# Attention on one core: VectorE's copy of the transposed x before another small block, two sets of small steps on later tiles

## What is computed

```python
q, k, v = x @ Wq, x @ Wk, x @ Wv                      # x: 16 sequences of 512 rows, 128 wide
latent_kv = (k + v) @ W_down_kv
k_rec, v_rec = latent_kv @ W_up_k, latent_kv @ W_up_v
scores = (q_heads @ k_heads.T) * scale                # 512 x 512 for each of 16 heads
scores = scores * exp(-1e-4 * |i - j|)
out = softmax(scores) @ v_heads
return concat_heads(out) @ Wo
```

## Time and profile before

| what | us |
|---|---|
| median of 3 runs | 1317.2 |
| lowest and highest | 1317.09, 1326.12 |
| the profiled execution, its own time | 1316.34 |
| its span, first to last instruction | 1314.3 |
| mean granted TensorE clock | 0.968 of full speed |

### The profile page before, as it was taken

One profiled execution on the slowest core, in us unless ns is written; L12 is line 12 of the kernel. 1 busy time (PEld: TensorE's weight loads), 2 busy tenths in 40 slices (PEclk: granted clock), 3 DMA queues, 4 the chain that ended last, 5 costly groups with the idle time before them and its releaser, 6 DMA issues. The chain is left out here.

```text
span 1314.3 us, 27474 instructions
## 1 busy us (share of the span) xinstructions
PE 1172.5 (89%) x7406; PEld 524.3 (40%) x7406; DVE 940.5 (72%) x2964; ACT 928.4 (71%) x1411; POOL 653.5 (50%) x1101
## 2 busy tenths in 40 slices
PE   4979999999999999996899749899969999999995
PEld 1222222222222222222566549577733443434442
DVE  5676777777777776776688766566466888888764
ACT  3878999999999999996665671445535666666554
POOL 5435555555555666423555540234233566666534
PEclk7999999999999999998999969899989999999998
DMA  5664565555566554511960003000000000000001
GB/s 155 138 122 88 90 115 108 105 103 105 104 116 114 110 105 96 103 34 59 236 193 11 1 5 125 1 1 0 0 0 1 9 9 16 16 8 17 9 17 33
DMA packets 71699, 87.96 MB, mean 67 GB/s; under 512 B 10368, under 2 KB 65190, under 8 KB 66022
## 3 DMA queue, kind: packets, MB, share of 16 engines
q1 hardware_dynamic: 69326, 85.81, 30.9%
q10 hardware_dynamic: 2296, 1.25, 0.4%
HBM read 63.84 MB, written 31.59 MB: 73 GB/s over the span
## 5 line engine op out<-in xcount | busy, mean ns | idle before, releaser
L562 ACT ACTIVATE a_probs<-a_S 128x1024 f32<-128x1024 f32 x512 | 496.8, 1037 | 53.7 <-DVE a_S L708 46.2
L708 DVE TENSOR_TENSOR a_S<-a_S,a_tables 128x256 f32<-128x256 f32 (+1 forms) x512 | 281.3, 561 | 149.1 <-PE a_S L578 146.1
L585 PE MATMUL a_O<-a_probs,a_V 128*32 128x512 f32 x2048 | 275.9, 611 | 2.4 <-ACT a_probs L562 0.6
L578 PE MATMUL a_S<-a_Qs,a_Ks 48*128 48x512 bf16 x1024 | 180.8, 390 | 15.8 <-ACT a_probs L562 10.5
L578 PEld LDWEIGHTS a_S<-a_Qs,a_Ks 48*128 48x128 bf16 x1024 | 42.7, 93 | 231.5 <-ACT a_probs L562 195.0
L2276 ACT ACTIVATE e_hid<-e_H 128x512 f32<-128x512 f32 x128 | 69.5, 595 | 57.6 <-PE e_H L2391 57.6
L455 POOL CAST a_parts<-a_whole 128x512 bf16<-128x512 f32 x45 | 27.5, 612 | 151.7 <-DVE a_whole L718 151.7
L1962 ACT ACTIVATE g_hid<-g_H,w_b 128x512 f32<-128x512 f32 x64 | 44.0, 687 | 57.9 <-PE g_H L1996 57.9
L2389 PE MATMUL e_H<-e_gated,w_We 64*128 64x512 f32 x256 | 73.2, 648 | 1.3 <-ACT e_hid L2276 1.2
L585 PEld LDWEIGHTS a_O<-a_probs,a_V 128*32 128x32 f32 x2048 | 40.5, 108 | 82.9 <-issue 67.8
L2400 PE MATMUL e_O<-e_hid,w_We 128*64 128x512 f32 x256 | 68.7, 609 | 0.4 <-ACT e_hid L2276 0.4
(11 more groups left out here) (405 smaller groups left out, 2382.1 us busy)
## 6 DMA issues: line engine op xcount, KB each, us to landing
a_parts_dram<-a_parts SPq DMA_DIRECT2D x94, 192.0 KB, 5.5
a_Qs<-a_parts_dram SPq DMA_DIRECT2D x60, 192.0 KB
m_taps_by_step<-h_taps SPq DMA_DIRECT2D x8, 1024.0 KB, 13.6
m_taps<-m_taps_by_step SPq DMA_DIRECT2D x8, 1024.0 KB, 5.1
a_Qs<-a_parts_dram SPq DMA_DIRECT2D x60, 128.0 KB
a_Ks<-a_parts_dram SPq DMA_DIRECT2D x30, 192.0 KB
a_Qs<-a_parts_dram SPq DMA_DIRECT2D x68, 64.0 KB
XY<-L_attn_x SPq DMA_DIRECT2D x16, 256.0 KB, 7.2
```

Source lines behind the costliest of these rows:

```text
L562: act.activation(probs[n % KEPT][:], S[n % RING][:], ACT.Exp).then_inc(exped, 1)
L578: mm = pe.matmul(S[n % RING][:, par, :], Ks[p][rows, pr, kb * P:(kb + 1) * P], Qs[p][Q_OF(kb)][rows, pr, :], start=True, stop=True)
L585: mm = pe.matmul(O[VC * j:VC * (j + 1), :], V[q][:, kb, HG * g + j, :], probs[(2 * m + j // 2) % KEPT][:, j % 2, :], start=(kb == 0), stop ...
L708: v.tensor_tensor(s[:, :, where], s[:, :, where], wide, ALU.mult).then_inc(corrected, 1)
```

## The change

On VectorE, within a batch: the copy of xT is done after the correction of tile 19 in place of tile 20; the small steps of `joined` move from tile 19 to tile 28; the four `bn_stats` of `next_norm`, with the wait ahead of them, move from tile 21 to tile 24, where its small steps follow them at once. No instruction is added or removed, and no other engine's order is touched.

```diff
@@ -873,11 +873,9 @@
                         out_norm.moments_of(v, t - 1, None, p=1 - p)
                     if n == 11 and (not isinstance(t, int) or t >= 2):
                         out_norm.moments_of(v, t - 2, None, p=p)
-                    if n == 21 and (not isinstance(t, int) or t >= 2):
+                    if n == 24 and (not isinstance(t, int) or t >= 2):
                         out_norm.wait_added(v, t - 2)
-                        next_norm.moments_of(v, t - 2, X[:, t - 2], only_stats=True, p=p)
-                    if n == 24 and (not isinstance(t, int) or t >= 2):
-                        next_norm.moments_of(v, t - 2, None, core.xmean, p=p)
+                        next_norm.moments_of(v, t - 2, X[:, t - 2], core.xmean, p=p)
                     if n in (16, 22, 31):
                         g = (n - 16) // 6
                         invert(at(f"OT{g}"), g, t * 2 + 1 if g == 0 else None)
@@ -887,10 +885,10 @@
                     if n == 18 and ahead and (not isinstance(t, int) or t < B - 3):
                         v.wait_ge(later[1 - p], (t - p) * 8 + 32)
                         joined.moments_of(v, t + 3, X[:, t + 3], only_stats=True, p=1 - p)
-                    if n == 19 and ahead and (not isinstance(t, int) or t < B - 3):
+                    if n == 19 and ahead:
+                        take(at("xT"), xnT[:])
+                    if n == 28 and ahead and (not isinstance(t, int) or t < B - 3):
                         joined.moments_of(v, t + 3, None, core.in_mean, p=1 - p)
-                    if n == 20 and ahead:
-                        take(at("xT"), xnT[:])
                     if n == 25 and ahead:
                         scale_queries(at("q"), t + 2)
                     if n == 29 and ahead:
```

## The result

The changed kernel took 1311.18 us (median of 8 runs, 1309.06 to 1313.5). The kernel before, run beside it, took 1323.17 us (median of 8, 1317.09 to 1326.21). The ratio is 0.9925, with a 95% interval from 0.9905 to 0.9945. The change makes the kernel faster, by 10 to 12 us (the ratio says 9.9, the two medians are 12.0 apart) and less than 1%. Two later comparisons of the same pair gave 0.991 (0.9882 to 0.9939) and 0.9921 (0.9891 to 0.995). The forecast was 11.9 us, 0.9%, and 1305.3 us. That time is 5.9 us too low: it rested on a median of three runs of the kernel before, 1317.2, and the median of eight was 6.0 us higher.

The account below looks back on a forecast made before the run. Prediction: no engine fills a batch; engines waiting for each other in a ring lose some 2.6 us of it. 2.6 + 9.9 + 0.2 - 0.8 = 11.9 us gave 1305.3 us for the median; range 1301.5 to 1311.5.

Parts of the forecast that it names:

- Batches 2 to 12: Copy one tile ahead and small steps away from tile 19: 0.90 us a batch, 9.9 us in eleven batches.
- The stall: TensorE's 1.20 us wait before OT1 (L601) in batch 7 for the copy of xT, claimed to go whole.
- the ring: Score, correction, exponential, and three tiles on the next score: claimed to limit score 24's gain to 0.82 to 0.90 us.
- The statistics at tile 24: Block of 1.54 to 1.7 us ahead of correction 25, claimed covered by the q projection with 0.3 to 0.5 us spare.
- Batches 14 and 15: No q projection, so no cover for the statistics block: 0.4 us lost in each, 0.8 in all.
- Batches 13, 0 and 1: Batch 13 gains 0.2 us; batch 0's gain is lost to batch 1's key wait; batch 1 gains 2.6 us.
- Its low clock: Batch 1's 3.41 us at clock 0.50 behind its 2.31 us stall, claimed to go, worth 1.7 us.
- rival 1: Start of batch 2: second low stretch, 111.65 to 115.06, goes too, about 1.4 us more, 1303.9 us; chance 0.20.
- All behind the attention is unchanged and starts sooner by the same amount: Layers after the attention: claimed to pass the 11.9 us gain on unchanged.
- The absolute time: Whole kernel: profiled execution 1304.4 us, plus 0.9 for the median of the runs, 1305.3 us.
- rival 3: Ring bound elsewhere, only small steps leaving tile 19 count: eleven times 0.6 less 0.8, 5.8 us, 1311.4; chance 0.12.
- rival 4: Statistics block ahead of correction 25 becomes the bound: 14 times 0.4, 5.6 us lost, 1322.8 us; chance 0.05.

Follow-up runs that it names:

- swap: Against the kernel before: copy of xT to tile 19 and small steps of `joined` to tile 20, statistics as before; 1315.61 us, ratio 0.9941.
- small_only: Against the kernel before: only the small steps of `joined` moved to tile 28, copy at tile 20, statistics at tile 21; 1309.9 us, ratio 0.9932.
- stats_only: Against the kernel before: only the statistics of `next_norm` moved from tile 21 to tile 24; 1323.17 us, ratio 1.003.
- before_b: The kernel before run again, nothing changed; profiled execution 1319.76 us, ratio to the kernel before 0.9996.
- before_c: The kernel before run a third time, nothing changed; profiled execution 1317.43 us, ratio to the kernel before 1.0.
- stats_kept: Against the changed kernel: statistics of `next_norm` left at tile 21, their small steps at tile 24; 1309.51 us, ratio 0.9907.
- stats_twice: Against the changed kernel: four more bn_stats that nothing reads, ahead of the statistics at tile 24; 1321.46 us, ratio 1.0002.
- q_later: Against stats_kept: q projection behind score 25 instead of 24, scaling of the queries split over tiles 26 and 27; 1316.52 us, ratio 0.9958.

## Why the prediction was right or wrong

**Batches 2 to 12: right.** Eleven times 0.90 was forecast, 9.9 us. Batches 3 to 11 are shorter by 0.88 to 0.91, batch 12 by 0.76, batch 2 by 0.88 against the profiles that have no low stretch in it: 9.7 us. The stall goes whole, score 24 is then late by ScalarE, and score 25 follows after TensorE's own work, as walked; swap (stall gone, half the gain) and small_only (stall shortened, most of the gain) tell the ring from the stall.

**The statistics at tile 24: covered, but the term was mis-sized.** "Ends at 318.14 to 318.30 ... with 0.3 to 0.5 us to spare" was wrong: the block measured 1.94 us to the end of its last step in the changed kernel (308.85 to 310.79), and the same in stats_only, where correction 25 starts 1.88 us after it begins; VectorE was idle 0.09 us before correction 25 of the changed kernel. It cost nothing in the changed kernel, 0.15 us a batch in stats_only. The fault was to take the length from a row outside the loop, where the block is 0.34 us shorter.

**Batches 14 and 15: direction right, size too large.** 0.4 us each was forecast, 0.25 and 0.23 measured. Exponential 25 did come 0.41 us later (a step of 1.31 in place of 0.90 us), but 0.18 of it came back before exponential 31 (a step of 1.37, now 1.19), which in both kernels waits for its correction, whose score stands behind the transposes of OT2. I had looked only at the place of the loss.

**Batches 13, 0 and 1.** Batch 13 gained 0.16 for 0.2. Batch 0 gained nothing: 38.28 and 38.39 us, and batch 1 still begins with a wait for keys, 3.22 us before and 3.74 in the changed kernel. Batch 1 went from 42.29 to 40.16, 2.1 for 2.6. Its low clock went: the fall to 0.50 at 96.7 to 98.8 us is in all five profiles with the copy at tile 20 (before, before_b, before_c, small_only, stats_only) and in none of the nine with the copy at tile 19. TensorE's stall there is 2.30 or 2.31 us in four of the five and 1.68 in small_only, 0.70 in the changed kernel, and the clock behind that is full (the timeline of TensorE, and the window that answers to the earlier trace rows):

```profile
96.10 0.63 PE L601 MATMUL a_M<-ident,a_Osb 128*128 128x128 f32 x4 [0.70 <-DVE a_xnT L712]
```

```profile
97.90:101.30 3.40, 3.11 (x22) 0.76 (x18) 2.12 (x8) 3.40 (x4) 0.00 (x0) 1.00 0.13 24
```

The Trainium skill's rule on gaps (page "TensorE: Matmul & The Clock Gate", section "HAM oscillation — how this bites in real kernels") speaks of longer ones, and the measurement decides against it as I read it: a stall of 1.68 to 2.31 us among the light work of this batch came with a fall each time, and one of 0.70 us never. The stalls of 1.2 us in batches 3 to 11 came with none, so the work around a stall counts too; how much of it, no run separates. But the clock did not only give: at the start of batch 1 it was at 0.50 for 6.8 us in place of 3.4, and tile 0 took 2.42 us in place of 1.55. That isn't shown to be the change: tile 0 took 2.40 us in before_b, and 1.56 in stats_kept.

**The second low stretch (rival 1).** It is gone as well, batch 2 took 34.72 in place of 37.10. But it isn't in every execution with the copy at tile 20: before_b, before_c and stats_only have no fall near 112 us, and batch 2 takes 35.6 us in the first two. small_only has one (batch 2 took 36.38 us). So it is in two of five profiles with the copy at tile 20 and in none of nine with it at tile 19. The 1.5 us that it cost are in the 12.9 us of the profiled pair by luck of which executions were profiled.

**"All behind the attention is unchanged and starts sooner by the same amount": this is the step that failed.** The sum of 11.9 us has no term for what lies behind the attention; the range had two microseconds for it at its low end alone, as a gain. The attention became 12.9 us shorter in the profiled pair, but only 10.0 us were left where the last layer starts, and 2.8 at the end: 9.0 us were lost in the three layers behind it. The code is unchanged; its time isn't a constant. The layers between took about 2 us more in each of three profiles, for a cause that stays open. The mean clock over the first 31 us of the last layer was 0.89, 0.68 and 0.89 in the profiles of the kernel before and 0.52, 0.83 and 0.89 in those of the changed one, and from 0.89 to 0.52 is 7 us. The ratio over the runs, 0.9925, 0.991 and 0.9921, says 10 to 12 us, while the attention's own part is 10.4 to 12.9 by which two profiles are compared, 11.7 by their means. That 11.9 lies within all this is no proof of its terms: batch 1, batches 14 and 15 and the second low stretch missed in both directions and nearly cancelled.

**The absolute time.** 1305.3 was the forecast difference put on the median of the three runs shown. Those were two near 1317.1 and one at 1326.12, so it was one of the two ends of a wide spread, and medians of eight and more runs put the kernel before at 1317.4 to 1323.2. The 6.0 us from 1317.2 to 1323.17 are all of the 5.9 us by which 1305.3 was too low. It is the same fault: I took the time of the unchanged code for one number. The third run should have been read as the sign of that. The comparisons ran on different chips as well (medians of the kernel before 1322.6, 1318.75, 1320.79 and 1317.48 on four of them); chip and chance aren't separated here. The low end of the range, 1301.5, is a slip too: 1303.9 less two is 1301.9.

**Halves (rival 3) and slower (rival 4).** Both fell. Small steps alone give 0.75 us and not 0.6, and the copy gives 0.15 more; and the q projection did keep TensorE long enough. stats_twice shows how near rival 4 was: 0.16 us of room.

What decides whether the last layer gets the long low stretch stays open. TensorE stands still for 2.9 us before that layer in both profiles and waits often in its first 31 us (it is busy 23.4 of them before, 23.9 in the changed kernel).

## What to carry to other kernels

Where engines hand buffers round in a ring, walk the ring tile by tile with starts and hand-on times of the profile; take away a stall and name the next one, for it sets the gain (here 0.9 of the 1.2 us, and 0.45 when only the stall went). Take the length of a block from rows in the same loop and beside the same work of other engines, and look down the rest of the round for where a loss is won back. Before a forecast of under 1%, look at every stretch of low clock in the profile, also in layers that don't change: what one of them is worth can be larger than the edit.

## What the runs showed of the hardware that I had not expected

**Small steps held up beside GpSimd.** At tile 28 the third small step of `joined` (L161) took 0.41 us instead of 0.17, and the five of them 1.05 us instead of 0.80 (from the start of the first to the end of the last). The trace of the changed kernel by source line (number of instructions, min/median/max in ns), and the timeline of batch 7 there:

```profile
L161 DVE SCALAR_TENSOR_TENSOR in_mean<-a_joined_diff,xst x16: 165/416/462, 5.5 to 488.3; 128x4 f32 x10, 128x4 f32<-128x4 f32 x6
...
L161 DVE SCALAR_TENSOR_TENSOR xmean<-next_diff,xst x16: 165/166/167, 136.7 to 629.2; 128x4 f32 x10, 128x4 f32<-128x4 f32 x6
```

```profile
314.36 0.61 POOL L461 CAST a_parts<-a_whole 128x512 bf16<-128x512 f32 x1 [0.17 <-POOL a_whole L458]
314.58 0.41 DVE L161 SCALAR_TENSOR_TENSOR in_mean<-a_joined_diff,xst 128x4 f32 x1
```

The step begins within GpSimd's cast and ends with it (314.97 and 314.99). In all 13 batches that have it at tile 28 it overlaps that cast and takes 0.41 to 0.46 us; in the kernel before, where GpSimd is idle at tile 19, it takes 0.17. The same instruction for `next_norm`, at tile 24 with GpSimd idle, stays at 0.17. The Trainium skill (page "SBUF — State Buffer", section "Who interferes with whom") says that a VectorE instruction with two inputs in SBUF contends with a GpSimd instruction that reads SBUF, and that the order of issue decides which of the two is blocked; the trace agrees. In q_later it agrees for two steps: L155 ends at 317.72, with GpSimd's instruction of L458 (316.55 to 317.71), and L161 at 318.50, with its cast (317.87 to 318.48). In the changed kernel the one long step left 0.14 us of the 1.09 us of cover at tile 28, not 0.35, and when q_later took the rest of that cover, ScalarE stood 0.94 us.

**The clock of one stretch differs from execution to execution.** In the last layer one and the same code ran at a mean clock of 0.89, 0.83, 0.68 or 0.52 over its first 31 us, for 355.2, 357.0, 359.2 and 362.4 us. The spread is in both kernels, though 0.52 was not seen in the three profiles of the kernel before.
